# Macaron block on one core: products with the values in pairs of groups, four buffers of probabilities, stacks in three rotating slots, other placing of the fills

## The reference, cut to what matters

```python
x = L0_attn_x                                    # (8, 1024, 256) float32
x = x + 0.5 * ffn(layernorm(x), ...)             # 8 experts, top 2 of them per token
x = x + attn(layernorm(x), Wq, bq, Wkv, bkv, Wo, bo)
x = x + 0.5 * ffn(layernorm(x), ...)

def attn(x, ...):                                # 16 heads of 16 columns
    q = x @ Wq.T + bq; k, v = split(x @ Wkv.T + bkv)
    dots = einsum('bhid,bhjd->bhij', q * 0.25, k)     # causal mask
    return einsum('bhij,bhjd->bhid', softmax(dots), v) @ Wo.T + bo

def ffn(tokens, ...):
    probs = softmax(x @ gate_w.T); top2_w, top2_idx = top_k(probs, 2)
    counts = bincount(top2_idx)                  # an expert with counts > cap = 1280 is dropped
    ...
```

## Time and profile before

| what | value |
|---|---|
| median of 3 runs | 1394.63 us (1393.09 to 1396.85) |
| the profiled execution | 1394.48 us |
| its span, first to last instruction | 1392.7 us |
| mean granted clock of TensorE | 0.980 of 2.4 GHz |
| PE, DVE, ACT, POOL busy | 1265.0, 1095.3, 941.5, 397.6 us |
| one step of a batch in the middle, hg 0 to 3 | 43.3, 42.6, 37.9, 37.8 us |

### The profile page before, as it was taken

One profiled execution on the slowest core, in us unless ns is written; L12 is line 12 of the kernel. 1 busy time (PEld: TensorE's weight loads), 2 busy tenths in 40 slices (PEclk: granted clock), 3 DMA queues, 4 the chain that ended last, 5 costly groups with the idle time before them and its releaser, 6 DMA issues.

```text
span 1392.7 us, 24439 instructions
## 1 busy us (share of the span) xinstructions
PE 1265.0 (91%) x8356; PEld 547.7 (39%) x8356; DVE 1095.3 (79%) x3527; ACT 941.5 (68%) x1697; POOL 397.6 (29%) x508
## 2 busy tenths in 40 slices
PE   3879999999999999999999999999999999998973
PEld 2323334443344433443344433444344533433332
DVE  5788888778888888878887788878888788779643
ACT  2257776777767677767767777676777677666661
POOL 3223322332323322232323232233223323221120
PEclk9899999999999999999999999999999999999897
DMA  4480433542425433244435423154342234330000
GB/s 139 90 169 13 69 69 57 99 86 56 72 36 99 89 68 69 47 80 84 69 58 99 97 53 71 28 99 96 61 69 56 51 73 69 68 58 31 1 16 19
DMA packets 57832, 95.17 MB, mean 68 GB/s; under 512 B 8352, under 2 KB 51488, under 8 KB 51744
## 3 DMA queue, kind: packets, MB, share of 16 engines
q1 hardware_dynamic: 55664, 92.30, 35.1%
q10 hardware_dynamic: 2032, 1.19, 0.3%
HBM read 59.91 MB, written 33.55 MB: 67 GB/s over the span
## 4 chain that ended last, share of the span: by engine, by line
PE 59%; DVE 17%; ACT 12%; issue 5%; POOL 3%; DVEq 2%; DMA 2%; SPq 1%; POOLq 0%; ACTq 0%
PE o_bank L1225 15%; PE s L1206 13%; PE st L1191 11%; PE misc L1141 7%; ACT q_stack L796 5%; DVE s L953 5%; ACT probs L809 5%; PE misc L1167 4%; PE misc L1136 4%; DVE max_full L957 3%; PE misc L497 3%; POOL probs L682 1%; DVE o_tok L1043 1%; DVE stats L464 1%; PE misc L488 1%
## 5 line engine op out<-in xcount | busy, mean ns | idle before, releaser
L809 ACT ACTIVATE probs<-st 128x512 f32<-128x512 f32 (+1 forms) x1216 | 633.3, 582 | 199.8 <-PE st L1191 109.2
L953 DVE CUSTOM_DVE_ANT_0 s<-s,causal 128x128 f32<-128x128 f32 (+3 forms) x1024 | 494.8, 502 | 140.9 <-PE s L1206 138.1
L1206 PE MATMUL s<-k_stack,q_stack 96*128 96x512 bf16 (+3 forms) x1536 | 490.9, 332 | 38.3 <-DVE max_full L957 12.2
L1191 PE MATMUL st<-q_stack,k_stack 108*128 108x512 bf16 (+3 forms) x1536 | 485.7, 329 | 24.2 <-ACT probs L809 21.6
L957 DVE TENSOR_REDUCE max_full<-s 128x1 f32<-128x512 f32 x512 | 350.0, 684 | 30.8 <-PE s L1206 29.4
L1225 PE MATMUL o_bank<-probs,v_aug 128*17 128x512 f32 (+3 forms) x3072 | 325.7, 496 | 8.8 <-POOL probs L682 6.5
L682 POOL TENSOR_SCALAR_AFFINE_SELECT probs<-probs 128x512 f32<-128x512 f32 x256 | 163.7, 644 | 535.0 <-ACT probs L809 534.8
L1206 PEld LDWEIGHTS s<-k_stack,q_stack 96*128 96x128 bf16 x1536 | 148.9, 98 | 394.8 <-DVE max_diag L953 178.1
L1191 PEld LDWEIGHTS st<-q_stack,k_stack 108*128 108x128 bf16 x1536 | 149.3, 98 | 145.3 <-ACT probs L809 54.9
L694 POOL TENSOR_TENSOR qk<-qk,parts 128x512 f32<-128x512 f32 x64 | 74.2, 1159 | 318.4 <-ACT parts L769 318.4
L953 DVE DVE_READ_ACCUMULATOR2_ANT max_diag<- 128x1 f32 x1024 | 144.8, 141 | 0.0
(11 more groups left out here) (107 smaller groups left out, 859.9 us busy)
## 6 DMA issues: line engine op xcount, KB each, us to landing
part_dram<-parts SPq DMA_DIRECT2D x128, 192.0 KB, 2.8
k_stack<-part_dram SPq DMA_DIRECT2D x186, 128.0 KB, 7.0
q_stack<-part_dram SPq DMA_DIRECT2D x31, 384.0 KB, 5.0
x_all<-x SPq DMA_DIRECT2D x16, 512.0 KB, 10.6
q_stack<-part_dram SPq DMA_DIRECT2D x31, 256.0 KB, 7.4
out<-x_all SPq DMA_DIRECT2D x7, 1024.0 KB, 11.1
q_stack<-part_dram SPq DMA_DIRECT2D x33, 128.0 KB, 8.8
k_stack<-part_dram SPq DMA_DIRECT2D x12, 64.0 KB, 2.9
```

Of the source, the lines that this page charges most:

```text
L809: nc.scalar.activation(probs[:, g % 2, h - part:h + 1, 0:width], st_bank[i % 3][:, 0:share * width] .rearrange("p (h c) -> p h c", c=width ...
L953: nc.vector.tensor_tensor_reduce(out=bank, in0=bank, in1=causal[:, CW - width:CW], scale=1.0, scalar=-BIG, op0=ALU.add, op1=ALU.max, accum ...
L1191: score = nc.tensor.matmul(st_bank[i % 3][:, part * width:(part + 1) * width], k_stack[0:KROWS + MROWS, hg, h, jb * P:(jb + 1) * P], q_sta ...
L1206: nc.tensor.matmul(s_bank[u % 3][:, 0:width], q_stack[0:KROWS, hm, h, ib * P:(ib + 1) * P], k_stack[0:KROWS, hm, h, j0:j0 + width], start= ...
```

## The change

`pv` is now issued for two groups at a time, at the first place of every odd group: groups g-3 and g-2 at u = 4, 12, 20, 28, 36 and 44. `probs` has four buffers, and the exponential of group g waits for `pv` of g-4. `oev` is at h = 3 of its group. The stacks go to three slots, `step % 3`, and the load of a stack is an event of its own, `stack`, at u = 1, two steps ahead. It waits until `st` of the step before has been done. The `ones` rows are written for three slots. `PLACE` is new for most fills.

```diff
+SLOTS = 3
+PBUF = 4
 PLACE = {
-    "v": (5, 9, 18, 21), "otr3": (1, 12), "qk3": (15, 24), "x_norm": (8, 24), "xt": (27, 30, 38, 44),
-    "bo": (8, 20, 28, 36), "ont": (1, 10, 20, 30), "wo": (7, 16, 25, 36), "otr0": (13, 33), "qk0": (4, 23),
-    "otr1": (0, 9), "qk1": (5, 26), "gate0": (4, 19, 23, 31, 36),
-    "otr2": (1, 9), "qk2": (5, 22), "gate1": (4, 18, 26, 31, 37),
-    "end": (24, 26, 29, 32, 35), "top2": 17, "before": ((12, 17), (12, 28)), "xload": 0, "top0": (2, 4), "count0": 2,
+    "v": (8, 16, 24, 40), "otr3": (1, 11), "qk3": (0, 32), "x_norm": (8, 24), "xt": (26, 30, 38, 44),
+    "bo": (8, 20, 28, 36), "ont": (2, 10, 18, 26), "wo": (8, 16, 24, 32), "otr0": (14, 35), "qk0": (0, 40),
+    "otr1": (1, 10), "qk1": (8, 24), "gate0": (4, 18, 22, 31, 34),
+    "otr2": (1, 10), "qk2": (8, 24), "gate1": (4, 18, 22, 31, 35),
+    "stack": 1, "end": (25, 27, 29, 32, 34), "top2": 17, "before": ((12, 17), (12, 28)), "xload": 0, "top0": (2, 4), "count0": 2,
     "total0": 7, "pro_v": (1, 3), "pro_qk": (8, 17, 26, 35, 44, 53), "pro_before": (5, 12),
     "mtr": ((33, 40), (39, 42), (14, 40), (14, 42)),
 }
-OEV_AT = 0
+PV_AT, OEV_AT = 0, 3
+def slot(step):
+    return step % SLOTS
+    if hg == 1 or (prev if hg == 0 else nxt):
+        put(PLACE["stack"], ("stack", (hg + 2) % NG))
-            if h == 0 and not (hg == 0 and not prev and g < 2):
-                plan.append(("pv", (g - 2) % NGRP))
+            if h == PV_AT and g % 2 == 1 and not (hg == 0 and not prev and g == 1):
+                plan += [("pv", (g - 3) % NGRP), ("pv", (g - 2) % NGRP)]
-    plan += [(3, "ones", hq) for hq in range(NG)] + [(3, "use", "v", j) for j in range(2)]
+    plan += [(3, "ones", i) for i in range(SLOTS)] + [(3, "use", "v", j) for j in range(2)]
-        q_stack = sb("q_stack", [P, NG, HG, S], BF16)
-        k_stack = sb("k_stack", [P, NG, HG, S], BF16)
+        q_stack = sb("q_stack", [P, SLOTS, HG, S], BF16)
+        k_stack = sb("k_stack", [P, SLOTS, HG, S], BF16)
-        probs = sb("probs", [P, 2, HG, CW])
+        probs = sb("probs", [P, PBUF, HG, CW])
+            def load_stack(sig, step):
+                hq, at = step % NG, slot(step)
+                for half in range(2):
+                    eng.wait_ge(sig.parts_out[half], 32 * (step + 1))
+                wait(eng, sig.st_full, NSB * (step - SLOTS + 1))
+                for r, times, part in RUNS:
+                    ...  # the nine DMAs as before, into slot `at`
-                    elif c == 1:
-                        ...
-                        wait(eng, sig.pv_done, lin(b, NGRP * m[0], NGRP * (m[1] - 3)))
-                        ...
+                    elif b < 0 and c == 1 and hq < SLOTS:
+                        load_stack(sig, hq)
+                elif kind == "stack":
+                    load_stack(sig, NG * b + hg + 2)
-                        wait(eng, sig.pv_done, lin(b, NGRP * NG, NGRP * hg + g - 1))
+                        wait(eng, sig.pv_done, lin(b, NGRP * NG, NGRP * hg + g - PBUF + 1))
```

More of the change, by code:

```diff
@@ L568, in moe_sync @@
                 moe_experts(eng, layer, None, None, expert)
+            def load_stack(sig, step):
[4 more added lines that the diff above has]
+                for r, times, part in RUNS:
+                    rows = slice(r * HD, (r + times) * HD)
+                    eng.dma_start(q_stack[rows, at, :, :].rearrange("r h c -> r (h c)"),
+                                  part_dram[hq, 0, 0:times, :, :].rearrange("k (d h) c -> (k d) (h c)", h=HG))\
+                       .then_inc(sig.stack_in[hq], 16)
+                    for copy in range(times):
+                        rows = slice((r + copy) * HD, (r + copy + 1) * HD)
+                        eng.dma_start(k_stack[rows, at, :, :].rearrange("r h c -> r (h c)"),
+                                      part_dram[hq, 1, part, :, :].rearrange("(d h) c -> d (h c)", h=HG))\
+                           .then_inc(sig.stack_in[hq], 16)
             def handle(sig, b, n, hg, kind, *a):
@@ L590, in handle @@
                                 rows = slice((r + copy) * HD, (r + copy + 1) * HD)
-                                eng.dma_start(k_stack[rows, hq, :, cols],
+                                eng.dma_start(k_stack[rows, slot(0), :, cols],
                                               part_dram[hq, 1, part, :, cols].rearrange("(d h) c -> d h c", h=HG))\
                                    .then_inc(landed, 16)
-                    elif c == 1:
-                        for half in range(2):
-                            eng.wait_ge(sig.parts_out[half], lin(b, 32 * m[0], 32 * m[1] + 32))
-                        wait(eng, sig.pv_done, lin(b, NGRP * m[0], NGRP * (m[1] - 3)))
-                        for r, times, part in RUNS:
-                            rows = slice(r * HD, (r + times) * HD)
-                            eng.dma_start(q_stack[rows, hq, :, :].rearrange("r h c -> r (h c)"),
-                                          part_dram[hq, 0, 0:times, :, :].rearrange("k (d h) c -> (k d) (h c)", h=HG))\
-                               .then_inc(sig.stack_in[hq], 16)
-                            for copy in range(times):
-                                rows = slice((r + copy) * HD, (r + copy + 1) * HD)
-                                eng.dma_start(k_stack[rows, hq, :, :].rearrange("r h c -> r (h c)"),
-                                              part_dram[hq, 1, part, :, :].rearrange("(d h) c -> d (h c)", h=HG))\
-                                   .then_inc(sig.stack_in[hq], 16)
+                    elif b < 0 and c == 1 and hq < SLOTS:
+                        load_stack(sig, hq)
+                elif kind == "stack":
+                    load_stack(sig, NG * b + hg + 2)
                 elif kind == "xload":
@@ L679, in handle @@
                         eng.wait_ge(sig.exp_done, lin(b, NSB * NG, NSB * hg + exps_through(g)))
-                        now = probs[:, g % 2, :, 0:P]
+                        now = probs[:, g % PBUF, :, 0:P]
                         nc.gpsimd.affine_select(out=now, in_=now, compare_op=ALU.is_ge, fill=0.0, base=0,
@@ L1205, in handle @@
                     wait(eng, sig.max_done, lin(b, NU * NG, NU * (hg + ahead) + u - 2))
-                    nc.tensor.matmul(s_bank[u % 3][:, 0:width], q_stack[0:KROWS, hm, h, ib * P:(ib + 1) * P],
-                                     k_stack[0:KROWS, hm, h, j0:j0 + width], start=True, stop=True)\
+                    nc.tensor.matmul(s_bank[u % 3][:, 0:width], q_stack[0:KROWS, at, h, ib * P:(ib + 1) * P],
+                                     k_stack[0:KROWS, at, h, j0:j0 + width], start=True, stop=True)\
                         .then_inc(sig.s_full, 1)
@@ L1226, in handle @@
                                                 v_aug[:, jb, of % NG * HG + h, :],
-                                                probs[:, g % 2, h, 0:CW - off], start=g in (0, CT),
+                                                probs[:, g % PBUF, h, 0:CW - off], start=g in (0, CT),
                                                 stop=g in (CT - 1, NGRP - 1))
```

17 lines of the change are left out of this document (8 added, 9 removed).

## The result

The changed kernel takes **1540.6 us** (median of 4 runs, 1537.6 to 1542.8), beside 1394.0 of the kernel before: ratio 1.105, 95% interval 1.104 to 1.106. The forecast was 1410 us, with a range from 1376 to 1432. The direction was right and the size wrong by 131 us.

The account below looks back on a forecast made before the run. PE's own work, busy 91%, was taken as the bound, with DVE's maxima and the single misc bank close behind. Span 1392.7 + 19 (middle batches) + 0 - 2.5 - 1.5 = 1407.7, so 1410 us measured; range 1376 to 1432.

Parts of the forecast that it names:

- I take 38: PE, `pv`: 191 pairs each save 0.20 us of going in and out, 38 us less; bounds 0 and 38.
- `oev` moves three places back: nothing: ACT's copy of `o_bank`: the next `pv` needing it is five places behind, ACT's queue idles 10 us a step; no cost.
- The turns of the misc chain: Single misc bank: PE stands when fills follow too soon; sums 3.35 us in hg 0, 4.85 less 0.5 in hg 1.
- The idle times of now, all of which I let go: PE's idle in hg 0 and 1 of a middle batch, 1.8 and 1.3 us, subtracted in full against the turns.
- +0.35: hg 0 of a middle batch, in us: turns 3.35, less idle 1.8, less 1.2 for six pairs.
- 1.85: hg 1 of a middle batch, in us more: 4.35 of turns, less idle 1.3, less 1.2 for pairs.
- +0.5 for each: hg 2 and hg 3 of a middle batch: 0.5 us more each, bounds -0.8 and +1.4, as PE has slack there.
- DVE and ACT starve: Rival, chance 0.08: a third of a batch's 24 pairs loses 0.5 us more, a batch 4 us; 1434 us.
- The sign that the prediction gave for it: PE's weight loads waiting for DVE's maxima much longer than now would speak for starving.
- The ends: First batch 0, last batch -2.5 us, prologue -1.5 us from three ones rows instead of four.
- DMAs cost nothing: Same nine loads a stack, now at place 1, needed at place 33, two thirds of 38 us away: nothing.
- 1433 us: Rival, chance 0.04: pairs save nothing, the second group goes in and out as now; 1433 us.

Follow-up runs that it names:

- the old places: Changed kernel with the fills' `PLACE` table of before, `"stack": 1` added; pairs, four buffers and three slots kept: 1435.3 us.
- both engines light: DVE's maxima over a quarter, ACT's exponentials over half of the columns: changed kernel 1391.9 us; with fills placed as before, singles 1333.3, pairs 1332.7.
- The kernel with one moved fill in hg 0 and 1: Single `pv` groups, fills placed as before, only the first half of the `qk` projection moved to place 0 of steps 0 and 1: 1410.4 us.
- light DVE: Only DVE's maxima over a quarter of their columns: changed kernel 1411.9 us; with fills placed as before, single groups 1358.7, pairs 1378.1.
- single groups on the old places: Changed kernel with `pv` one group at a time, `oev` at h = 0 and the `PLACE` of before; four buffers, three slots kept: 1390.3 us.
- single groups on the new places: Changed kernel with `pv` one group at a time and `oev` at h = 0; its fill places, buffers and slots kept: 1504.1 us.

## Why the prediction was wrong

**The pairs: size of the edges right, value wrong.** The step "I take 38" was right about PE's work (0.19 us a pair measured, 0.20 forecast). It was wrong in counting them as time: at full work, with their later copy, they cost 45 us on the old places and 36 on the new ones. With both engines light they give 22.7 us on the new places, and 0.6 on the old ones, where PE's waits for that copy eat them. So a part of the 38 us is there when the other engines keep up. At full work they do not: a group's `pv` every four places was also the time in which DVE and ACT emptied their banks. In pairs it comes in one piece every eight places, and in between PE asks for eight maxima and eight exponentials in a row.

**"`oev` moves three places back: nothing" was wrong**, by 16 us on the old places. The prediction asked when `o_bank` is needed again, and not who reads `o_raw`: the transpose at place 9 does, and ACT has the evictions of `qk` in front of the copy. In the changed kernel the transpose at place 10 waits for these evictions first, and PE's wait for `o_raw` is 2.7 us in the whole run; what the later copy costs there was not tried.

**The turns of the misc chain: priced right.** Five of them were measured within 0.15 us. A sixth, `v` and `mtr` at place 40 of hg 0, was priced at 0.85 and took 0.75, and the one at place 10 of hg 2 and 3, priced at 1.1, took 0.67 in hg 2, behind a slow fill, and 1.03 in hg 3. The largest miss is 0.2 us, at place 16 of hg 1 (0.65 for 0.45). What follows the turns failed, not their sizes.

**"The idle times of now, all of which I let go" was wrong.** The two steps idled 1.8 and 1.3 us. They idle 49.70 - 42.68 = 7.0 and 47.20 - 41.17 = 6.0 now. A turn does not use up the slack of its step, since the slack is at other places. The kernel with one moved fill in hg 0 and 1 shows it alone: its two turns of 1.10 us cost 2.9 us a batch, and nothing was given back from the 3.1 us of idle time.

**hg 0, "+0.35", was missed by the most.** It went from 43.3 to 49.7 us. Its three turns are 3.1 us of idle time, where 3.35 were priced. Beside them PE stands 3.2 us in six waits for DVE's maxima, and the `v` fill at place 8 takes 1.5 us longer; neither is in the sum. hg 1 went up by 4.6 instead of 1.85.

**"+0.5 for each" of hg 2 and 3 was wrong too.** They went from 37.9 and 37.8 us to 42.8 and 41.2. The trace had shown that DVE works without a pause from 636.18 to 653.00, and the `qk` fill stood in this stretch. The prediction priced its move by the turn it makes behind, and not by what it covered in front. Putting it back gave 41 us.

**The rival "DVE and ACT starve" was the right mechanism** with a chance of 0.08 and a price of 24 us. The price rested on a third of the pairs losing 0.5 us. The kernels with light DVE put it at 97 of the 150 us between single groups on the old places and the changed kernel. The sign that the prediction gave for it, longer waits of the weight loads for the maxima, did not come: they fell from 286.8 to 270.6 us, while PE's own waits rose from 21 to 71.

**Without starving the forecast still misses.** With both engines light the same change costs 58.6 us: places 81.3, pairs -22.7. The prediction had +53 for the places and the rest, and -38 for the pairs, 15 in all. The changed kernel with light DVE takes 1411.9 us, close to the 1410, and its middle batch with both engines light takes 164.4 us where 161.6 + 3.2 = 164.8 was forecast. That is luck: the sum starts from the kernel before at full work, and light engines make a kernel on the old places faster too. By step it is off in both directions (45.2, 45.2, 37.0 and 37.0 instead of 43.6, 44.4, 38.3 and 38.3).

**The ends.** The first batch, taken as 0, costs 14.0 us, and the last, taken as -2.5, costs 7.6. These are taken to be the same errors as in the middle; no run separates them. The prologue costs 1.3 instead of giving 1.5. That DMAs cost nothing was right: PE's wait for `k_stack` was 10.5 us in the kernel before and is 10.1 now.

**The sum, as it came out.** From single groups on old places: places 114, pairs 36, less 4 for buffers and slots, 146 in all. In the prediction the pairs were -38 with next to nothing against it, and the other terms +53. So of the 131 us that are missing 74 lie in the pairs and 61 in the places, less the 4 (83 and 52 if the pairs are taken first). How much of the 114 is the order of fills in hg 0 and 1 and how much hg 2 and 3 was tried for one fill each only; the rest of the split stays open. The range was also drawn short of its own rivals: they were priced at 1434 and 1433 us, its end is 1432.

## What to carry to other kernels

When PE is the bound at 91% and two engines stand at 79% and 68%, a product that needs no other engine is not only work: it can be the time in which the others catch up. Before moving or bundling such work, list at each place what the other queues do during it, and price the move by both ends, what it now delays behind and what it no longer covers in front. Bundling took its 27.8 us off PE's busy time, and the run got shorter by most of it only where DVE and ACT were light and no late copy was awaited; ask both before counting the edges as time. When a buffer is emptied later, ask not only when it is filled again, but who reads the copy.

## What the runs showed of the hardware

**The clock fell in some of the fills that come behind pauses.** Windows of the changed kernel: the stretch ahead of the `v` fill at 613.27, and the fill; and the `qk` fill at 707.88.

```profile
606.00:613.20 7.20, 4.20 (x36) 1.71 (x35) 5.26 (x15) 5.15 (x10) 3.58 (x4) 0.97 1.04 148
613.20:616.50 3.30, 3.30 (x9) 2.62 (x10) 1.43 (x6) 0.00 (x0) 0.00 (x0) 0.55 0.78 148
707.80:711.00 3.20, 3.18 (x6) 1.21 (x7) 2.39 (x12) 0.00 (x0) 0.00 (x0) 0.59 1.00 133
```

PE had stood 3.0 of 7.2 us, and then the granted clock is 0.55 over the fill: mostly 1.2 GHz instead of 2.4. There the pause is paid a second time. It does not happen behind each such pause. In hg 3 the same waits (0.26, 0.32 and 1.28 us) stand ahead of the fill, and it takes 1.94 us:

```profile
750.62 0.23 PE L1220 MATMUL s<-k_stack,q_stack 96*128 96x128 bf16 x1 [1.28 <-DVE max_full L972]
750.68 1.94 PE L1155 MATMUL misc<-x_t,w_qk 128*128 128x512 f32 x4
```

Over the run the fills of `v` take 438 ns a matmul instead of 388 and those of `qk` 667 instead of 605. Their busy time rises from 56.7 to 66.6 and from 111.9 to 125.4 us, 23 us in all. With single groups on the new places they take 391 and 608 ns, although PE waits 52 us for maxima there too. What makes the difference was not tried.

**Small operations of DVE stretch beside one of POOL.** In the changed kernel:

```profile
610.76 1.15 POOL L715 TENSOR_TENSOR parts<-qk,parts 128x512 bf16<-128x512 f32 x1 [0.52 <-DVE parts L1050]
610.77 1.18 DVE L987 CAST max_parts<-max_rest 128x16 bf16<-128x16 f32 x1
```

A cast of 16 columns, 0.17 us elsewhere, ends with POOL's operation that began with it, and `s` at 612.26 waits behind it. This cast took 226 ns on average before and 420 now:

```profile
L972 DVE CAST max_parts<-max_rest 128x16 bf16<-128x16 f32 x64 | 14.5, 226 | 5.8
```

```profile
L987 DVE CAST max_parts<-max_rest 128x16 bf16<-128x16 f32 x64 | 26.9, 420 | 6.5 <-issue 0.9
```

The Trainium skill, SBUF — State Buffer, section SBUF: two separate sides, says that DVE, in a mode that uses two ports or with two SBUF inputs, and GpSimd share a pair of ports which the first of them holds for its whole instruction while the other stands. The trace agrees, if the cast is in such a mode, which the trace does not tell: it lasts as long as POOL's 1.15 us. How much of the loss this makes was not tried by itself.
